# A twelve-stage transformer stack on one core: the 4-bit feed-forward with its constant step and LayerNorm on the scalar engine and its middle values a slot later, and the quantised layers' magnitude by the tensor engine

## What is computed

```
xn = (x - mu) * rsqrt(var + 1e-3) * ln_gamma + ln_beta      # of the LayerNorm of x
beta = mean(abs(weight));  w_q = clip(round(weight / (beta + 1e-5)), -1, 1)
gamma = max(abs(xn))                                        # over all tokens
xq = clip(xn * 128 / gamma, -128 + 1e-5, 128 - 1e-5)
y = (xq @ w_q) * (gamma * beta / 128)
```

```
def fp4(x):   # blocks of 16 along the last dimension
    scale = max(max(abs(x), axis=-1) / 6, 1e-12)
    return nearest_grid(abs(x / scale)) * sign(x) * scale
h = silu(fp4(x) @ fp4(w_gate).T) * (fp4(x) @ fp4(w_up).T)   # 128 -> 352
y = fp4(h) @ fp4(w_down).T                                  # 352 -> 128
```

## Time and profile before

| | |
|---|---|
| time, median of 3 runs | 4482.23 us (4474.24 to 4483.7) |
| the profiled execution's own time | 4482.93 us |
| its span | 4481.1 us |
| tensor engine busy | 3940.5 us |
| vector engine busy | 3417.1 us |
| scalar engine busy | 3078.3 us |
| GpSimd busy | 1492.7 us |
| mean granted clock of the tensor engine | 0.931 of full |

### The profile page before, as it was taken

One profiled execution on the slowest core, in us unless ns is written; L12 is line 12 of the kernel. 1 busy time (PEld: TensorE's weight loads), 2 busy tenths in 40 slices (PEclk: granted clock), 3 DMA queues, 4 the chain that ended last, 5 costly groups with the idle time before them and its releaser, 6 DMA issues.

```text
span 4481.1 us, 65524 instructions
## 1 busy us (share of the span) xinstructions
PE 3940.5 (88%) x15916; PEld 2209.6 (49%) x15916; DVE 3417.1 (76%) x10934; ACT 3078.3 (69%) x5687; POOL 1492.7 (33%) x2814
## 2 busy tenths in 40 slices
PE   5688869999999999999999999997688659999966
PEld 3466734444444444444444444443465447777744
DVE  5888579888888788788787887885767956665678
ACT  3454338999999899899899998996142226665632
POOL 2322124444444344344444444443111013333310
PEclk8788779999999999999999999999799769999987
DMA  2112010000000000000100000000000001111100
GB/s 58 29 29 42 16 24 1 1 22 3 16 10 1 20 6 1 20 6 1 25 1 16 10 1 21 5 1 1 0 1 0 0 16 45 42 44 42 44 3 16
DMA packets 152079, 71.92 MB, mean 16 GB/s; under 512 B 109576, under 2 KB 142684, under 8 KB 151666
## 3 DMA queue, kind: packets, MB, share of 16 engines
q1 hardware_dynamic: 144738, 63.96, 5.8%
q10 hardware_dynamic: 6928, 3.41, 0.2%
HBM read 54.55 MB, written 12.80 MB: 15 GB/s over the span
## 4 chain that ended last, share of the span: by engine, by line
PE 61%; DVE 18%; ACT 11%; issue 7%; DMA 1%; POOL 1%; DVEq 0%; ACTq 0%; SPq 0%; POOLq 0%
PE bank L1909 20%; PE bank L1924 7%; PE bank L2693 5%; PE bank L1953 5%; PE bank L1963 3%; PE bank L2726 2%; PE bank L613 2%; DVE arena L1356 2%; ACT L2047 2%; DVE arena L1360 2%; ACT arena L2001 2%; ACT arena L2004 2%; ACT arena L2000 2%; ACT arena L2013 2%; PE bank L2753 1%
## 5 line engine op out<-in xcount | busy, mean ns | idle before, releaser
L1909 PE MATMUL bank<-arena 128*128 128x512 f32 x3072 | 1424.9, 597 | 12.5 <-issue 7.9
L1909 PEld LDWEIGHTS bank<-arena 128*128 128x128 f32 x3072 | 587.6, 192 | 759.3 <-issue 732.4
L2150 POOL TENSOR_SCALAR arena<-arena 128x256 f32<-128x256 f32 x1024 | 481.9, 481 | 1197.2 <-DVE arena L2083 1197.2
L1924 PE MATMUL bank<-arena 128*128 128x512 f32 x1024 | 526.8, 606 | 65.3 <-DVE arena L2113 65.1
L2072 DVE SCALAR_TENSOR_TENSOR arena<-arena 128x256 f32<-128x256 f32 x1024 | 393.3, 420 | 200.5 <-ACT arena L2001 194.2
L2113 DVE SCALAR_TENSOR_TENSOR arena<-arena 128x256 f32<-128x256 f32 x1024 | 491.3, 524 | 14.5 <-issue 14.5
L2090 DVE SCALAR_TENSOR_TENSOR arena<-bank,bv,arena 128x256 f32<-128x256 f32 x1024 | 444.8, 472 | 0.0
L2000 ACT ACTIVATE arena<-bank,bqk 128x512 f32<-128x512 f32 x512 | 348.0, 680 | 81.8 <-PE bank L1909 70.8
L2083 DVE SCALAR_TENSOR_TENSOR arena<-bank,bq,arena 128x512 f32<-128x512 f32 x512 | 384.1, 750 | 18.1
L2013 ACT ACTIVATE arena<-arena,const_table 128x512 f32<-128x512 f32 x512 | 374.4, 731 | 0.0
L2004 ACT ACTIVATE arena<-bank,bqk 128x512 f32<-128x512 f32 x512 | 353.6, 691 | 1.5 <-PE bank L1909 1.5
(11 more groups left out here) (368 smaller groups left out, 7365.6 us busy)
## 6 DMA issues: line engine op xcount, KB each, us to landing
arena<-packed_dram SPq DMA_DIRECT2D x96, 96.0 KB
arena<-packed_dram SPq DMA_DIRECT2D x32, 288.0 KB
arena<-diag_dram SPq DMA_DIRECT2D x16, 256.0 KB, 3.9
arena<-in_L_attn_Wk_dram SPq DMA_DIRECT2D x16, 256.0 KB, 3.3
arena<-in_L_attn_Wq_dram SPq DMA_DIRECT2D x16, 256.0 KB, 4.1
arena<-in_L_attn_Wv_dram SPq DMA_DIRECT2D x16, 256.0 KB, 4.5
arena<-in_L_attn_Wo_dram SPq DMA_DIRECT2D x8, 512.0 KB, 3.7
arena<-in_L_attn_W_dram SPq DMA_DIRECT2D x16, 256.0 KB, 2.7
```

Source lines behind the costliest of these rows:

```text
L1909: nc.tensor.matmul(bank[:, RING1[m % 5], :], w1p[k][:, i * P:(i + 1) * P], zT_of(g), start=True, stop=True).then_inc(a1_proj.sem, 1)
L1924: nc.tensor.matmul(bank[:, 6, :], wo1[:, i, :], a1_att[:, i % 4, :], start=(i == 0), stop=(i == NB1 - 1)).then_inc(a1_outd.sem, 1)
L2150: last = nc.gpsimd.tensor_scalar(a, a, 1.0, a1_ksum[:, i % 4, b:b + 1], ALU.add, ALU.mult)
```

## The change

Quantised layer: the maximum over partitions is made by a transpose of the column into one row of PSUM (bank 4), a vector maximum over that row, and a product of a row of ones with the result, which puts it on all partitions (bank 5). The weight's sum over partitions is a product with a matrix of ones. PARTITION_ALL_REDUCE is no longer used.

4-bit feed-forward: `apply_dve` becomes `apply_act`, Identity with scale rstd and bias -mean * rstd, the bias made by two small GpSimd instructions. The exponent mask and its scaling go; the rounding constant is now Abs(v * 2^22) on the scalar engine, written in bf16, and the floor of 2^22 * (1 + 2^-7) is the first operation of two scalar_tensor_tensor (max, then add; max, then subtract). Scales are kept negative, which turns the sign of the product back. x and h have buffers of their own. On the vector engine h is worked on three slots after the statistics and the add comes four after; the order in a slot alternates between h and x. The up products and the turns of h are split so that they alternate on the tensor and scalar engines. The weights' rounding stays as it was.

```diff
@@ quantised layer
-                dve.wait_ge(f1_top, rep + 1)
-                steps = [ ...
+                dve.wait_ge(f1_top, 2 * rep + 1)
+                nc.vector.tensor_reduce(f1_s[0:1, 1:2], bank[0:1, 4, 0:P], AX.X, ALU.max).then_inc(f1_scale, 1)
+                dve.wait_ge(f1_top, 2 * rep + 2)
+                nc.vector.reciprocal(f1_s[:, 2:3], bank[:, 5, 0:1]).then_inc(f1_scale, 1)
...
-            def scale_pool(pool):
-                pool.wait_ge(f1_scale, 4 * rep + 1)
-                nc.gpsimd.partition_all_reduce(f1_s[:, 1:2], f1_s[:, 0:1], P, bass.bass_isa.ReduceOp.max)\
+            def scale_pe(pe):
+                pe.wait_ge(f1_scale, 5 * rep + 1)
+                nc.tensor.transpose(bank[0:1, 4, 0:P], f1_s[:, 0:1], ident).then_inc(f1_top, 1)
+                pe.wait_ge(f1_scale, 5 * rep + 2)
+                nc.tensor.matmul(bank[:, 5, 0:1], ones[0:1, :], f1_s[0:1, 1:2], start=True, stop=True)\
                     .then_inc(f1_top, 1)
@@ the weight's sum
-            def ffn1_weights_pool(pool):
-                pool.wait_ge(f1_wsum, 1)
-                nc.gpsimd.partition_all_reduce(w1s[:, 1:2], w1s[:, 0:1], P, bass.bass_isa.ReduceOp.add)\
+            def ffn1_weights_pe(pe):
+                pe.wait_ge(f1_wsum, 1)
+                nc.tensor.matmul(bank[:, 5, 2:3], ones, w1s[:, 0:1], start=True, stop=True).then_inc(f1_wall, 1)
@@ 4-bit feed-forward
+            def apply_act(g, u):
+                f3_bias.wait(nc.scalar, g + rep * G)
+                xt_psum.wait_free(nc.scalar, g + n * G)
+                for q in range(QT):
+                    last = nc.scalar.activation(xn[:, u, q, :], tile(g, q), ACT.Identity,
+                                                bias=f3_nb[:, u, q:q + 1], scale=rstd[:, u, q:q + 1])
...
+            def h_abs_act(g, u):
+                f3_hstep.wait(nc.scalar, g + rep * G, 5)
+                nc.scalar.activation(f3_hm[:], f3_hv[:], ACT.Abs, scale=STEP_MAGIC).then_inc(f3_habs.sem, 1)
+
+            def h_round_dve(g, u):
+                s = g + rep * G
+                f3_habs.wait(nc.vector, s)
+                nc.vector.scalar_tensor_tensor(f3_hv[:], f3_hm[:], STEP_LEAST, f3_hv[:], ALU.max, ALU.add)\
+                    .then_inc(f3_hstep.sem, 1)
+                f3_hstep.wait(nc.vector, s, 6)
+                nc.vector.scalar_tensor_tensor(f3_hv[:], f3_hm[:], STEP_LEAST, f3_hv[:], ALU.max, ALU.subtract)\
+                    .then_inc(f3_hstep.sem, 1)
...
             programs["vector"].append(lambda e: over_groups(
-                e, [(0, stats_dve), (1, apply_dve), (1, quant_x_dve), (2, quant_h_dve), (3, add_dve)]))
-            programs["gpsimd"].append(lambda e: over_groups(e, [(0, rstd_pool)]))
+                e, [(3, h_product_dve), (0, stats_dve), (3, h_norm_dve), (1, x_norm_dve), (3, h_round_dve),
+                    (1, x_round_dve), (4, add_dve), (3, h_scale_dve)]))
+            programs["gpsimd"].append(lambda e: over_groups(e, [(0, rstd_pool), (0, bias_pool)]))
             programs["tensor"].append(lambda e: over_groups(
-                e, [(0, transpose_pe), (0, up_pe), (1, down_pe)], gate(e, n)))
+                e, [(0, transpose_pe), (0, up_pe((0, 1))), (2, turn_pe(0)), (2, turn_pe(1)), (0, up_pe((2, 3))),
+                    (2, turn_pe(2)), (2, down_pe)], gate(e, n)))
             programs["scalar"].append(lambda e: over_groups(
-                e, [(0, copy_act), (0, silu_act), (1, copy_h_act)], gate(e, n)))
+                e, [(2, copy_act), (2, silu_act((0, 1))), (4, copy_h_act(0)), (4, copy_h_act(1)),
+                    (2, silu_act((2, 3))), (3, h_abs_act), (4, copy_h_act(2)), (1, x_abs_act), (0, apply_act)]))
```

More of the change, by code:

```diff
@@ L770, in silu_act @@
-            def silu_act(g, u):
-                s = g + rep * G
-                if n and isinstance(g, int) and g == 0:
-                    x_written.wait(nc.scalar, n * G - 1)
-                f3_mul.wait_free(nc.scalar, s)
-                for q in range(QT):
-                    f3_up.wait(nc.scalar, s, q + 1)
-                    nc.scalar.activation(f3_silu[:, u, q, :], bank[:, 2 + 2 * (q % 2), 0:FF3], ACT.Silu)
-                    nc.scalar.activation(f3_upc[:, u, q, :], bank[:, 3 + 2 * (q % 2), 0:FF3], ACT.Copy)\
-                        .then_inc(f3_act.sem, 1)
@@ L781, in quant_h_dve, with up_pe, fn @@
-            def quant_h_dve(g, u):
+            def up_pe(qs):
+                def fn(g, u):
+                    s = g + rep * G
+                    xt_ready.wait(nc.tensor, g + n * G)
+                    if n and isinstance(g, int) and g == 0:
+                        x_written.wait(nc.tensor, n * G - 1)
+                    for q in qs:
+                        f3_act.wait_free(nc.tensor, s, q + 1)
+                        nc.tensor.matmul(bank[:, 2 + 2 * (q % 2), 0:FF3], xT_tile(u, q), wgT[:], start=True, stop=True)
+                        nc.tensor.matmul(bank[:, 3 + 2 * (q % 2), 0:FF3], xT_tile(u, q), wuT[:], start=True, stop=True)\
+                            .then_inc(f3_up.sem, 1)
+                return fn
@@ new lines, in silu_act, with fn @@
+            def silu_act(qs):
+                def fn(g, u):
+                    s = g + rep * G
+                    if qs[0] == 0:
+                        if n and isinstance(g, int) and g == 0:
+                            x_written.wait(nc.scalar, n * G - 1)
+                        f3_mul.wait_free(nc.scalar, s)
+                    for q in qs:
+                        f3_up.wait(nc.scalar, s, q + 1)
+                        nc.scalar.activation(f3_silu[:, u, q, :], bank[:, 2 + 2 * (q % 2), 0:FF3], ACT.Silu)
+                        nc.scalar.activation(f3_upc[:, u, q, :], bank[:, 3 + 2 * (q % 2), 0:FF3], ACT.Copy)\
+                            .then_inc(f3_act.sem, 1)
+                return fn
```

174 lines of the change are left out of this document (113 added, 61 removed).

## The result

The changed kernel takes **4423.43 us** (median of 4 runs, 4422.76 to 4430.31) where the kernel before takes 4479.2 us in the same comparison: ratio 0.9879, 95% interval 0.9862 to 0.9896, thus some 54 us less (47 to 62). The profiled execution took 4422.76 us, its span is 4421.0 us, against 4481.1 before: 60.1 us less in the two profiles. That is more than the 54, since the profiled execution before (4482.93 us) is near the slow end of its kernel and the profiled one after is the fastest of its own.

The account below looks back on a forecast made before the run. The vector engine's own instructions were taken to bound the 4-bit feed-forward; 35.2 us from its two uses and 15.0 from the quantised layers, off 4482.9, gave 4432.7, set at 4432 for the median, range 4416 to 4458.

Parts of the forecast that it names:

- What bounds the stage: 4-bit feed-forward: the vector engine's own instructions set the stage, 20.65 us busy of 22, with 12.3 us waiting at its ends.
- Durations: 4-bit feed-forward instructions: scalar_tensor_tensor at 1408 1.625 us, Abs 1.37 and 0.63, Identity 0.482, normalisation 1.15 a group.
- rival (c): Scalar engine's tables change between Silu and Abs, about 1 us a slot shows: 4449 us; chance 0.06.
- rival (e): 4-bit feed-forward: fewer waits at the ends, or a faster bf16 form of scalar_tensor_tensor: 4418 us; chance 0.10.
- The slot: 4-bit feed-forward: 3.92 us a group off the vector engine, about 21.9 falling to 18.0, saving 31.4 us per use.
- The ends: 4-bit feed-forward's pipeline ends: waits grow from 12.3 to 26.1 us per use, 13.8 more, leaving a gain of 17.6.
- The 8.8 of the last wait: End of each 4-bit feed-forward use: the vector engine's last wait was to remain 8.8 us.
- Room for the add: Feed-forward slot: down product ends just ahead of the final add, about 0.5 us of room; 1 us waits per use allowed.
- rival (b): Late tensor clock pushes silu and down product past the feed-forward's add, 1.5 us a slot, 24 us: 4457; chance 0.15.
- rival (a): Tensor clock stays at 1.2 GHz throughout the new feed-forward slot, 22.3 us a slot: 4500 us; chance 0.04.
- The quantised layer: Replacing the all-reduce gains 0.6 us per use, 7.6 after the second use, 6.2 after the first: 15.0 us.
- no MODIFY_POOL_CONFIG: Sign in the new profile: GpSimd is no longer reconfigured, and L287 starts within 0.3 us of the statistics.

Follow-up runs that it names:

- 5: The changed kernel with the 4-bit feed-forward's normalisation back on the vector engine as four tensor_scalar and GpSimd's small bias step gone: 4432.34 us, ratio 0.9894.
- 10: The changed kernel with semaphore waits making each part of the vector engine's feed-forward slot wait for the end of the part ahead: 4444.08 us, ratio 0.9913.
- 9: The changed kernel with 20 unused identity transposes per 4-bit feed-forward group on the tensor engine, ahead of the down product: 4420.8 us, ratio 0.986.
- 11: The changed kernel with both Abs magnitudes of the 4-bit feed-forward written in 32 bits instead of bf16: 4428.11 us, ratio 0.988.
- e2: The kernel before with only the 4-bit feed-forward's part of the change, the PARTITION_ALL_REDUCE kept: 4442.6 us, ratio 0.993.
- e4: The changed kernel with a PARTITION_ALL_REDUCE on GpSimd in each quantised layer whose result nobody uses: 4441.46 us, ratio 0.9922.
- 3: The kernel before, all-reduce kept, with one small unused GpSimd instruction right behind each scale PARTITION_ALL_REDUCE: 4465.84 us, ratio 0.998.
- experiment 7: The changed kernel with the 4-bit feed-forward's down product computed twice for two of the four tiles of every group: 4437.0 us, ratio 0.9911.

## Why the prediction was right, and where it was off

**What bounds the stage: right.** The vector engine sets the slot before and after; 5 and 10 put time on it and find it in the slot (1.15 us for 1.15); 9 makes the down product 1.5 us shorter and the slot stays.

**Durations: right.** scalar_tensor_tensor at 1408 was taken at 1.625 and is 1.623; Abs 1.37 and 0.63, measured 1.377 and 0.630; Identity 0.483; the normalisation's 1.15 is e5's. There is one table load per use and none in the loop, so rival (c) did not come. The part of rival (e) on bf16 is refuted by 11.

**The slot: mis-sized.** 18.0 forecast, 16.87 measured. The term that was off is "a slot of about 21.9 falls to 18.0": it took durations away and left the joints as they were. (The prediction's own order of the slot adds up to 17.7 us, part by part, where it gives 18.0.) Timeline of the kernel before, vector engine, its joints:

```profile
4376.53 0.69 DVE L684 TENSOR_TENSOR arena<-arena 128x512 f32<-128x512 f32 x1
...
4379.11 1.62 DVE L675 TENSOR_REDUCE arena<-arena 128x88 f32<-128x1408 f32 x1
...
4388.82 1.62 DVE L684 TENSOR_TENSOR arena<-arena 128x1408 f32<-128x1408 f32 x1
...
4390.62 0.69 DVE L825 SCALAR_TENSOR_TENSOR x<-bank,x 128x512 f32 x1 [0.18 <-DVE arena L684]
```

From L684 to L825 are 1.80 us, from L684 at 512 to L784 0.83, from L784 to L675 1.75. In the changed slot a 1408-wide instruction with an independent one behind it takes 1.53 (4310.08 to 4311.61), with a dependent one 1.66 (4311.61 to 4313.27); at 512 wide 0.60 against 0.72. Start to start, joint by joint: h_scale 1.80 to 1.53, product 1.75 to 1.66, and one overlap of 0.12 to 0.13 gained behind each of h_norm, x_norm and h_round, and 0.22 behind x_round: 0.96 us. This is the shorter half of the loop, 21.77 us; the longer one takes 22.0 to 22.2, its joints at h_scale and at the add being dearer still, and the mean is the 21.9. From the shorter one 21.77 - 3.92 - 0.96 = 16.89 follows, and that is the 16.87 measured. 10 shows that such overlap is worth time by taking it away, 1.74 us for eight joints, though not that it is worth 0.96.

**The ends: about right in size, for partly wrong reasons.** I forecast 12.3 us of waits growing to 26.1. With every joint of 0.15 us and more counted, they were 14.5 and 14.7 and are 28.6 and 29.9, so +14.6 instead of +13.8. The first x_norm (2.5, measured 2.62), x_abs (0.8, 0.69) and x_abs(1) (8.0, 7.6 and 7.98) came as worked out. In the two last slots the add waits 1.7 to 1.8 and the Abs another 1.44, where I had 2.5 for the add alone. The 4.28 at the last but one h_abs was missing, in the second use only (the first has 1.44): it stands behind a silu whose products ran at the half level. The 8.8 of the last wait fell to 6.7, since the product ran at the full level; the same code has 9.2 in the second use of e2 and of e4, so this is luck. Both are the clock at the ends, which I had weighed for the slot alone. Together: 4.4 us of work less per group and 14.6 more of waits, 20.6 us a use where I had 17.6, or 41.3 against 35.2.

**Room for the add: right by luck.** 0.5 us forecast; in the full slots the product ended 0.15 to 1.1 us ahead of the add, once 2.4. The product took 4.23 to 5.49 in the full slots, and once 2.94, not 4.67. In the first use rival (b) came at about a sixth of its price: the product ends with the slot, the add waits 0.19, and slots are 17.1 instead of 16.87. What I held against rival (a), that the half level had followed a stand of 6.73 us and the new slot had none so long, did not hold: the level was at half behind 3.56 us too. The rival stayed away because the level was back at full in each of these slots.

**The quantised layer: right.** 15.0 forecast, 14.9 found: 0.6 per use, 7.0 for 7.6 at the second, 6.7 for 6.2 at the first, where the weights are next late as foreseen. The stop belongs to the all-reduce and to the first ordinary instruction behind it (3 and 4). The sign "no MODIFY_POOL_CONFIG" came in part: at L287 the ten of the later stages are gone, and eight remain within the first 39 us, at the program's start. The Trainium skill's advice against this part (GPSIMD Engine Reference, "4.1 Engine selection") did not hold here: for one value per partition the tensor engine took 1.57 us where the way over GpSimd took 2.13, and the way over GpSimd cost two stops besides.

**The remainder.** 10 us of the difference of the two profiles were not forecast (60.1 against 50.2): 6.1 are the slots, less the ends, and some 4 lie in the second attention. Of these 2 or so belong to the first stop (experiment 4), the rest is within the spread of one execution. Against the 54 us of all runs, 50 forecast were only 4 short.

## What to carry to other kernels

When work is handed from the bounding engine to another, price the round trip first and look for independent work of the bounding engine to put in it; here the same operations in the plain order gave back all 54 us. Then price the joints, not only the durations: here an independent neighbour saved 0.12 us against a dependent one, and an added wait on one's own last result cost 0.22. Last, sum the waits at the ends of each pipeline use, and look at the tensor clock in just those microseconds: unused transposes in its pauses, two Abs moved ahead and one early table load were together worth another 12 us.

## What the runs showed of the hardware that I had not expected

- The first ordinary GpSimd instruction behind a PARTITION_ALL_REDUCE stands some 7 us (6.88 and 7.70 in experiment 3), unused or not, and can be spent where nobody waits.
- The same 24 small products take 2.94, 4.40 or 5.4 us by the granted clock. With a stand of 1.39 us it stayed full; behind stands of 2.2 to 3.9 us it was sometimes full and sometimes fell while the product was already running (experiment 9).
- More work can cost less than in proportion: 36 products took 5.91 us where 24 took 5.49 (experiment 7).
- Eight waits of the vector engine on its own results cost 1.74 us a slot without any work added (experiment 10).
